# A routing stage on one core: places, gates and scatter one turn later, and TensorE's way down ahead of the logits

## The reference, cut to what matters

```python
x = x + attn_a(layernorm(x)); x = x + ffn(layernorm(x))
x = x + attn_b(layernorm(x)); x = x + ffn(layernorm(x))

def ffn(x, Wr, Wg, Wu, Wd, Sg, Su, Sd):        # x: 16 x 512 x 128, T = 8192 tokens
    scores = softmax(xt @ Wr)                   # 8 experts
    topk_w, topk_idx = top_k(scores, 2)
    topk_w = topk_w / (topk_w.sum(-1) + EPS)    # the gates
    out_all = (silu(xt @ Wg) * (xt @ Wu)) @ Wd  # per expert; only the two chosen are used
    out = sum(out_all[topk_idx] * topk_w)
    shared = silu(x @ Sg) * (x @ Su) @ Sd       # the shared expert, for every token
    return out + shared
```

## Time and profile before

| | us |
|---|---|
| median of 3 runs | 3190.71 |
| lowest and highest | 3187.52 and 3202.62 |
| the profiled execution, its own time | 3181.02 |
| its span (first to last instruction) | 3179.0 |

### The profile page before, as it was taken

The page is one execution under the profiler, slowest core; times in us unless marked ns, Lnnn a source line. Parts: engine busy times, 40 slices in busy tenths (PEclk is TensorE's granted clock), DMA queues, the critical chain, the costliest instruction groups (busy, mean ns, idle before and its releaser), DMA issues.

```text
span 3179.0 us, 76627 instructions
## 1 busy us (share of the span) xinstructions
PE 2622.8 (83%) x26192; PEld 2124.4 (67%) x26193; DVE 2036.4 (64%) x5025; ACT 1808.9 (57%) x4422; POOL 853.9 (27%) x1042
## 2 busy tenths in 40 slices
PE   3999898988989997986886289999999978958882
PEld 2777777777777776775765166667666657857671
DVE  2777666776766765874554666666766647855555
ACT  2777777777777775552444265555665545534441
POOL 0000000000000002663555232342442315744551
PEclk9999999999999997666999599899999876669996
DMA  6323323332332221111222200000000001112225
GB/s 147 48 42 45 48 41 51 49 46 42 49 44 41 41 41 36 40 43 54 69 68 71 88 2 2 2 2 2 2 2 2 2 2 35 41 46 68 70 69 171
DMA packets 117817, 140.22 MB, mean 44 GB/s; under 512 B 21324, under 2 KB 79825, under 8 KB 117360
## 3 DMA queue, kind: packets, MB, share of 16 engines
q1 hardware_dynamic: 100592, 101.63, 17.2%
q0 software_dynamic: 16896, 34.12, 3.2%
HBM read 45.85 MB, written 40.54 MB: 27 GB/s over the span
## 4 chain that ended last, share of the span: by engine, by line
PE 50%; DVE 18%; issue 12%; ACT 9%; another core or an unknown queue 5%; DMA 2%; SPq 1%; DVEq 1%; POOL 1%; ACTq 0%; POOLq 0%
PE psum L457 5%; PE psum L426 5%; PE psum L492 4%; ACT probs L446 3%; PE psum L1515 3%; DVE state L1718 3%; DVE neg_max L435 2%; PE psum L1563 2%; DVE x_sb L1288 2%; PE psum L543 2%; PE psum L1137 2%; PE psum L1432 2%; PE psum L1125 2%; PE psum L304 2%
## 5 line engine op out<-in xcount | busy, mean ns | idle before, releaser
L446 ACT ACTIVATE probs<-psum,neg_max 128x512 f32<-128x512 f32 (+3 forms) x1024 | 539.8, 538 | 244.3 <-DVE neg_max L435 243.5
L435 DVE TENSOR_REDUCE neg_max<-psum 128x1 f32<-128x512 f32 (+3 forms) x1024 | 457.3, 483 | 54.0 <-PE psum L427 24.9
L426 PE MATMUL psum<-ls,qs 96*128 96x512 f32 (+3 forms) x1024 | 380.9, 397 | 112.4 <-ACT probs L446 96.5
L457 PE MATMUL psum<-ident,probs 128*128 128x128 f32 x2560 | 428.4, 283 | 2.9 <-ACT probs L446 0.8
L1250 POOL DMA_INDIRECT y_tok<-yb,xb x272 | 267.7, 984 | 301.5 <-DVE yb L1225 226.6
L426 PEld LDWEIGHTS psum<-ls,qs 96*128 96x128 f32 x1024 | 198.2, 194 | 216.8 <-ACT probs L446 158.4
L325 POOL TENSOR_TENSOR rstd<-var_eps,half_neg 128x4 f32<-128x4 f32 x32 | 40.1, 1254 | 1103.1 <-DVE var_eps L321 1103.1
L476 DVE COPY probs_t<-psum 128x512 f32<-128x512 f32 (+1 forms) x384 | 230.4, 600 | 147.5 <-PE psum L457 140.4
L457 PEld LDWEIGHTS psum<-ident,probs 128*128 128x128 f32 x2560 | 273.7, 144 | 26.1 <-ACT probs_t L472 10.1
L914 POOL DMA_INDIRECT x_slot<-pay,pos_i x256 | 256.3, 1001 | 129.8 <-issue 76.1
L427 PE MATMUL psum<-causal_r,ident_r 128*128 128x128 f32 x1024 | 235.4, 242 | 0.0
(11 more groups left out here) (320 smaller groups left out, 6748.8 us busy)
## 6 DMA issues: line engine op xcount, KB each, us to landing
qs<-q_h SPq DMA_DIRECT2D x128, 256.0 KB, 5.5
xb<-x_slot SPq DMA_DIRECT2D x272, 66.0 KB
qs<-q_l SPq DMA_DIRECT2D x64, 256.0 KB, 5.7
y<-y_tok SPq DMA_DIRECT2D x32, 512.0 KB, 3.5
y_tok<-yb,xb POOLq DMA_INDIRECT x272
x_sb<-in_x SPq DMA_DIRECT2D x16, 256.0 KB, 5.5
x_slot<-pay,pos_i POOLq DMA_INDIRECT x256
out<-x_sb SPq DMA_DIRECT2D x16, 256.0 KB, 2.9
```

The source lines that it names most:

```text
L426: pe.matmul(o[:, at:at + n], q, ls[par][0:3 * LD, 0:n], start=(at == 0), stop=False, skip_group_check=True)
L435: last = dve.tensor_reduce(neg_max[:, par, h, qt:qt + 1], bank[u % 3][:, at:at + (qt + 1) * P], AX.X, ALU.max, negate=True)
L446: last = act.activation(probs[:, u % 3, c], bank[u % 3][:, c], ACT.Exp, bias=neg_max[:, par, h, qt:qt + 1], accum_out=row_sum[:, par, h, q ...
L457: last = pe.transpose(bank[3 + u % 2][:, c:c + P], probs[:, u % 3, c:c + P], ident[:, :])
```

## The change

Nothing is added or taken away; the order changes on all four engines.

- DVE: places and gates of sequence b move from the end of turn b into turn b+1: the places to its very start, the gates between the shift and the scores. Those of sequence 15 stand behind the last turn.
- POOL: the scatter of b-1 is issued in turn b, behind rstd of b+3. Before, the scatter of b stood behind it.
- PE: the way down for b-1 comes ahead of the logits of b+1, the turn of b+2 and the place counts of b.
- ACT: the copy of the rows of b+2 stands ahead of the silus, and hi of b+2 ahead of the halves of the shared expert.
- The counts that waits on `r_step` compare with follow the new order (`steps_before`, `scored`); they are left out below.

```diff
@@ ffn_tensor, one turn
                     shared_up_tensor(pe, f, b, par, k)
+                if has_before(b):
+                    shared_down_tensor(pe, f, b - 1)
                 if left:
                     logits_tensor(pe, f, b + 1, 1 - par)
                 if left > 1:
                     route_turn_tensor(pe, f, b + 2, (slot + 2) % PAY_RING)
                 place_tensor(pe, f, b)
-                if has_before(b):
-                    shared_down_tensor(pe, f, b - 1)
@@ ffn_scalar, one turn
                     route_norm_scalar(act, f, b + 2, par, (slot + 2) % PAY_RING)
+                    route_copy_scalar(act, f, b + 2, (slot + 2) % PAY_RING)
                 for k in range(FC):
                     shared_silu_scalar(act, f, b, k)
+                if left > 1:
+                    route_hi_scalar(act, f, b + 2, par)
                 for k in range(FC):
                     shared_hi_scalar(act, f, b, k)
-                if left > 1:
-                    route_hi_scalar(act, f, b + 2, par)
-                    route_copy_scalar(act, f, b + 2, (slot + 2) % PAY_RING)
@@ ffn_vector, one turn
+                if has_before(b):
+                    place_vector(dve, f, b - 1, (slot - 1) % PAY_RING)
                 route_a_vector(dve, f, b)
                 if left:
                     route_lo_vector(dve, f, b + 1, 1 - par)
                 if left > 1:
                     route_shift_vector(dve, f, b + 2, par, *slot_after(slot, use, 2))
+                if has_before(b):
+                    gates_vector(dve, f, b - 1)
                 route_b_vector(dve, f, b)
                 if left > 2:
                     route_stats_vector(dve, f, b + 3, 1 - par)
                 for k in range(FC):
                     shared_mul_vector(dve, f, b, k)
-                place_vector(dve, f, b, slot)
-                gates_vector(dve, f, b)
@@ ffn_gpsimd, one turn
                 if left > 2:
                     route_rstd_gpsimd(pool, f, b + 3, 1 - par)
-                scatter_gpsimd(pool, f, b, slot)
+                if has_before(b):
+                    scatter_gpsimd(pool, f, b - 1, (slot - 1) % PAY_RING)
```

More of the change, by code:

```diff
@@ L715, in tile_x, with steps_before, scored @@
             return x_sb[:, bass.ds(t, 1), :].rearrange("p o d -> p (o d)")
+        FIRST_STEPS = 11
+        def steps_before(f, b):
+            if isinstance(b, int) and b == 0:
+                return f * SEQS * R_STEPS
+            return f * SEQS * R_STEPS + (b - 1) * R_STEPS + FIRST_STEPS
+        def scored(f, b):
+            return steps_before(f, b) + (2 if isinstance(b, int) and b == 0 else 4)
         def route_pairs(eng, batch):
@@ L798, in logits_tensor @@
             if not (isinstance(b, int) and b == 0):
-                pe.wait_ge(z["r_step"], (f * SEQS + b - 1) * R_STEPS + 2)
+                pe.wait_ge(z["r_step"], scored(f, b - 1))
             for t in range(QT):
@@ L806, in route_scalar @@
             z = fs
-            act.wait_ge(z["r_step"], (f * SEQS + b) * R_STEPS + 2)
+            act.wait_ge(z["r_step"], scored(f, b))
             act.activation(r_exp[:, :, :], r_log[:, :, :], ACT.Exp).then_inc(z["r_exped"], 1)
@@ L812, in route_a_vector @@
             logits = bank[6][:, 0:QT * E].rearrange("p (t e) -> p t e", t=QT)
-            n = (f * SEQS + b) * R_STEPS
+            n = scored(f, b) - 2
             dve.wait_ge(z["log_mm"], f * SEQS + b + 1)
@@ L822, in route_b_vector @@
             z = fs
-            n = (f * SEQS + b) * R_STEPS
+            n = steps_before(f, b) + (0 if isinstance(b, int) and b == 0 else 7)
             dve.wait_ge(z["r_exped"], f * SEQS + b + 1)
@@ L857, in gates_vector @@
             z = fs
-            n = (f * SEQS + b) * R_STEPS
+            n = steps_before(f, b + 1) + (2 if isinstance(b, int) and b == SEQS - 1 else 4) - 13
             dve.tensor_tensor(picked[:, :, :, :], pick[:, :, :, :],
@@ L878, in place_tensor @@
             if not (isinstance(b, int) and b == 0):
-                pe.wait_ge(z["r_step"], (f * SEQS + b - 1) * R_STEPS + 13)
+                pe.wait_ge(z["r_step"], steps_before(f, b) + 2)
             flat = chosen[:, :, :].rearrange("p t e -> p (t e)")
@@ L891, in place_vector @@
             z = fs
-            n = (f * SEQS + b) * R_STEPS
+            n = steps_before(f, b + 1) - 11
             dve.wait_ge(z["pos_mm"], f * SEQS + b + 1)
@@ L1364, in ffn_vector @@
             route_pairs(dve, batch)
+            place_vector(dve, f, SEQS - 1, (SEQS - 1) % PAY_RING)
+            gates_vector(dve, f, SEQS - 1)
             table_vector(dve, f)
@@ L1394, in ffn_gpsimd @@
             route_pairs(pool, batch)
+            scatter_gpsimd(pool, f, SEQS - 1, (SEQS - 1) % PAY_RING)
             moe_gpsimd(pool, f)
```

## The result

The changed kernel takes 3310.6 us (median; 3293.8 to 3330.7), the kernel before 3196.7 us beside it, a ratio of 1.036 [1.029, 1.043]. The profiled execution of the changed kernel took 3307.2 us, that of before 3181.0. The runs are from different chips, on which the kernel before takes 3046 to 3047 us or 3197 to 3207 us; a ratio is always to the kernel before timed on the same chip, and spans are compared across chips only where the text says so.

What follows compares the result with a forecast made beforehand. POOL's scatter was taken to pace the turn; the change closes a ring of 19.4 us instead of 13.49. With head and tail, 67 a stage, 134 for both, on 3181 gives 3315, plus 9.7 to the median: 3325 us, range 3288 to 3385.

Steps and rivals of the forecast that it cites:

- The ring: Routing stages: closed path from one turn's ids through var_eps, rstd and scatter to the next ids, 19.4 us a turn.
- scores and stats: DVE's work from the start of the scores to the end of var_eps, on the closed path: 4.95 us a turn.
- eight DMAs: POOL's issue of one scatter, on the closed path: 10.08 to 10.26 us, taken as 10.17.
- landing: From the scatter's end until DVE's wait ends: bounds 0 and 1.34 us, taken as 1.34, or 1.44 with DVE resuming.
- Twelve turns: Ids of turns 2 to 13 in each FFN stage wait for the scatter: 232.8 us instead of 161.9, +70.9.
- Head and tail: Each stage's start, turns 0 and 1, -1 us; its end, last ids to first block load, -3 us.
- the forecast's own range: Main case, chance 0.75: 3300 to 3355 us, allowing for rstd to first DMA, landing and tails.
- Late counts as well: Rival, 0.16: place counts visible only once the running scatter landed, so 1.8 us more per path, +44 us, 3369.
- Faster: Rival, 0.05: the ring's wait does not bite, turns fall to POOL's own 11.7 us, -43 us, 3148.
- no change: Rival, 0.04: scatter and landing take 5.7 us, or tail gains and a partly hidden ring cancel: 3190 us.
- PE's granted clock: Sign in the stage's profile: it should fall from 0.65, as PE's work spreads over a longer turn.

Runs made afterwards that it cites:

- twelve DMAs: Changed kernel with four extra indirect DMAs per scatter, twelve instead of eight, writing to memory nothing reads: 3371.8 us, ratio 1.109, a turn 24.2 us.
- the repeat: The changed kernel run once more, unmodified, on the second chip, against the kernel before: 3336.8 us, ratio 1.043, a turn 19.2 us.
- the scatter first: Changed kernel with POOL's scatter of b-1 put ahead of the rstd of b+3: 3028.3 us, ratio 0.994, and 0.995 when run again.

## Why the prediction was right

**The ring.** It held: the ids wait for a DMA, rstd waits for var_eps, and breaking either link (order or buffer) ends it. By its terms, from the turn shown above, in us:

| term | predicted | measured |
|---|---|---|
| ids to scores, with the gates | 0.14 + 1.36 | 1323.66 - 1322.22 = 1.44 |
| scores and stats to the end of var_eps | 4.95 | 1328.46 - 1323.66 = 4.80 |
| var_eps to rstd | 0.09 | 0.08 |
| rstd, and to the first DMA | 1.05 + 0.19 | 1329.79 - 1328.54 = 1.25 |
| eight DMAs | 10.17 | 1339.95 - 1329.79 = 10.16 |
| landing, and DVE resumes | 1.44 | 1341.48 - 1339.95 = 1.53 |
| a turn | 19.4 | 19.26; mean of 24: 19.15 |

The landing had no row of its own before. It was taken from the 1.34 us by which the late places followed a scatter, and it came out at 1.3 to 1.5, mostly 1.45 (1344.61 to 1346.06 with twelve DMAs; the turn shown has the longest). That the size was right is in part luck: the late places do not always follow the landing, as the last section shows, and with the other bound that the prediction names, 0, the turn would have been 18.0. The Trainium skill's "DMA: Bandwidth & Descriptors", anatomy of one DMA, gave an estimate of 1.2 us behind the issue's end for 66 KB; the trace has some 0.3 more, and the measurement decides.

**Twelve turns.** +67.75 and +68.1 us instead of +70.9: 0.25 us a turn too many, spread over scores and stats and over turns with a shorter path (18.8 to 19.5).

**Head and tail.** Predicted -1 and -3; measured -1.0 in both stages, and -1.6 and -2.7, from 57.97 to 1531.52 - 1475.10 = 56.42 us in the first. A stage came to +65.2 and +64.5 instead of +67. Both make 129.7, while the span grew by 126.3; the other 3.4 us lie outside the routing stages and were not looked into. The tail holds the two waits of DVE for PE, 3.45 and 8.23 us; it held two before as well, of 3.32 and 6.90.

**The sum.** 3181 + 134 = 3315 for the profiled execution stood against 3307.2; 3325 for the median against 3310.6, inside the forecast's own range. Of the 14 us between, 6 are the turns (24 x 0.25) and 6 the distance from profile to median, 9.7 before and 3.4 here, which differs from run to run; the rest is the 3.4 outside the stages, less 1.8 by which head and tail gained less than was said.

**Late counts as well** was wrong in turns 1 to 13, where the places have no wait, and right in turn 14, where the scatters run back to back: 3.45 us (3.0 and 2.9 in the repeat). The argument against it was that the counts would be recorded ahead of the scatter's start. They are, but the traces don't show that this is what kept the wait away. PE's last counts of the turn shown above, and those ahead of the places of turns 14 and 15:

```profile
1327.07 0.20 PE L898 MATMUL psum<-chosen,ones_bf 128*128 128x8 bf16 x2
...
1479.93 0.19 PE L898 MATMUL psum<-chosen,ones_bf 128*128 128x8 bf16 x2
...
1492.77 0.19 PE L898 MATMUL psum<-chosen,ones_bf 128*128 128x8 bf16 x2
```

The first end 2.5 us ahead of the scatter's first DMA (1329.79), and the places start at 1331.47 with no wait, while that scatter runs. The second end in the middle of one, whose last DMA is this:

```profile
1483.44 0.96 POOL L926 DMA_INDIRECT x_slot<-pay,pos_i  x1 [0.30 <-issue]
```

The places start at 1486.37, 6.25 us after the counts and 1.97 after the scatter. The third end in the middle of the next scatter (1488.19 to 1498.52) as well, and yet the places start 2.7 us later with no wait:

```profile
1495.68 0.18 DVE L906 TENSOR_TENSOR pos<-psum,run 128x32 f32<-128x32 f32 x1
```

So a count recorded while a scatter runs can be seen while it still runs. The new order also leaves some 4.2 us between the counts and the moment at which DVE asks for them, against 2.4 before (1325.27 less 1322.85), which by itself covers most of a delay of 4.5. Why this rival failed is open.

**Faster** and **no change** would have needed scatter and landing together under 3.6 or at 5.7 us. They are 11.7. Once the ring is open a turn is 11.5 us, near the 11.7 worked out for POOL's own work. That this is the gain of 43 us which the first named isn't shown: on those chips the kernel before has no profile, and the whole kernel gains only 17.5 to 18.5 us.

**PE's granted clock** was expected to fall and didn't (0.65, now 0.68). The step "as its work spreads over a longer turn" failed: PE is less busy (134 of 240 us against 146 of 162), and the clock granted is still a little higher. What the runs show is that PE's own order takes part: on the second chip the granted clock is 0.66 in the changed kernel and 0.62 with PE's part undone, where PE is busy for 157 of 240 us instead of 135 at the same turn. Why is open. It costs nothing, since PE isn't on the ring.

## What to carry to other kernels

Before an instruction is moved on an engine, write down for each buffer ring which engine frees it and what stands ahead of the freeing instruction there; if that waits for work behind the buffer's next writer, the ring closes and all terms add up in each turn. Order on the freeing engine or one more buffer opens it, and the same wait in a list cost nothing here where its releaser was never idle. A late semaphore in one stage of the present schedule says little about a schedule in which the same work is done at another moment.

## What the hardware showed unexpectedly

On the two chips where the kernel before takes 3046 us, no wait of DVE in the routing stages ends in "remote", in any of the eight profiles. On the chip of the first pair and on the second one it does: in the kernel before the places wait mostly 1.7 to 2.3 us a turn, with PE's part alone mostly 2.1 to 2.7. It isn't only the place counts: in the tail of the changed kernel the way down's last matmul ends at 1500.03, and its sum starts at 1510.96 after 8.23 us of waiting.

In 44 of the 52 waits at the places in the two profiles of the kernel before, the places start 1.1 to 1.7 us after the scatter's last DMA. This suggests a signal of PE's that becomes visible only when POOL's indirect DMAs have landed, but other turns of the same profiles speak against it. In five of the 52 the wait ends while the scatter's last DMA is still being issued, as here, at 1419.14 against 1419.29:

```profile
1418.33 0.96 POOL L914 DMA_INDIRECT x_slot<-pay,pos_i  x1 [0.30 <-issue]
```

```profile
1419.14 0.19 DVE L894 TENSOR_TENSOR pos<-psum,run 128x32 f32<-128x32 f32 x1 [1.82 <-remote]
```

And in the last turn the counts end at 1440.50 in the middle of a scatter, and the places start 0.94 us later with no wait, with three DMAs of that scatter still to come:

```profile
1440.31 0.19 PE L886 MATMUL psum<-chosen,ones_bf 128*128 128x8 bf16 x2
```

```profile
1441.44 0.18 DVE L894 TENSOR_TENSOR pos<-psum,run 128x32 f32<-128x32 f32 x1
```

So what holds these signals back, and why chips differ, stays open; no experiment on these two chips delayed the scatter without the counts.

The chips differ outside the routing stages as well. Between the profiled kernel with the scatter first (span 3028.3) and the changed one (3305.3) lie 277 us, of which the two stages hold 207; the other 70 lie in the rest of the kernel, which is the same code: some 38 us behind each stage, less 6 ahead of the first. The kernel before has no profile on the faster chips, so how its own 150 us divide is open too.
